# Routed experts on 23 tiles of gathered rows, in place of all eight experts over all tokens

## The reference

```python
# attention: 16 heads of 16, rope, each query picks 4 of 16 key blocks, softmax, RMS per head, @ Wo.T
# feed-forward over T = 1024 tokens, E = 8 experts, K = 2, H = 176
scores = softmax(x @ gate_w)
topk_w, topk_idx = top_k(scores, K)
comb = zeros((T, E)).at[arange(T)[:, None], topk_idx].add(topk_w)
g = silu(einsum('td,edh->teh', x, w_gate)) * einsum('td,edh->teh', x, w_up)
routed = einsum('teh,ehd,te->td', g, w_down, comb)
shared = silu(x @ sw_gate) * (x @ sw_up) @ sw_down      # width 352
out = routed + shared
```

## Time and profile before

| | us |
|---|---|
| median of the 3 runs shown | 426.15 (424.23 to 426.80) |
| span of the profiled execution, first to last instruction | 422.4 |
| layer 0's share of it, to the first transfer issue of layer 1 | 318.9 |
| TensorE, VectorE, POOL, ScalarE busy | 348.9, 300.3, 172.9, 170.7 |
| mean granted clock of TensorE, share of full | 0.935 |
| moved by transfers | 30.2 MB |

### The profile page before, as it was taken

One profiled execution on the slowest core, in us unless ns is written; L12 is line 12 of the kernel. 1 busy time (PEld: TensorE's weight loads), 2 busy tenths in 40 slices (PEclk: granted clock), 3 DMA queues, 4 the chain that ended last, 5 costly groups with the idle time before them and its releaser, 6 DMA issues. The chain is left out here.

```text
span 422.4 us, 6057 instructions
## 1 busy us (share of the span) xinstructions
PE 348.9 (83%) x2028; PEld 240.3 (57%) x2028; DVE 300.3 (71%) x857; ACT 170.7 (40%) x305; POOL 172.9 (41%) x119
## 2 busy tenths in 40 slices
PE   0697767668779989999999999999682888996881
PEld 0586555546546657676665665656581776444641
DVE  3867489867997877894444764684668859758794
ACT  1422453551224323226444445544212475956610
POOL 5654283473444642554256526664536000000023
PEclk9999689697999999999999999999966789999898
DMA  8300168987793311212211141110006100000011
GB/s 267 74 23 21 50 160 178 163 141 182 183 180 88 87 47 44 70 37 52 63 43 42 40 137 39 39 37 2 1 2 216 48 0 2 0 1 0 2 50 50
DMA packets 17009, 30.20 MB, mean 71 GB/s; under 512 B 3140, under 2 KB 12012, under 8 KB 16556
## 3 DMA queue, kind: packets, MB, share of 16 engines
q1 hardware_dynamic: 12946, 18.80, 19.2%
q10 hardware_dynamic: 4032, 11.01, 9.0%
HBM read 24.99 MB, written 4.82 MB: 71 GB/s over the span
## 5 line engine op out<-in xcount | busy, mean ns | idle before, releaser
L388 POOL TENSOR_TENSOR wl<-wr,wh 128x768 fp32r<-128x768 f32 x28 | 51.2, 1829 | 65.3 <-ACT wh L474 49.1
L530 ACT ACTIVATE PT<-bank 128x512 f32<-128x512 f32 (+1 forms) x88 | 44.3, 557 | 39.5 <-PE bank L952 39.4
L687 DVE TENSOR_REDUCE mx<-bank 128x1 f32<-128x384 f32 (+3 forms) x88 | 52.2, 635 | 7.2 <-PE bank L934 6.9
L149 PE MATMUL bank<-xh,wh 128*128 128x512 f32 x112 | 50.7, 452 | 4.0 <-DVE gb L812 1.4
L426 POOL TENSOR_TENSOR gl<-gb,gh 128x512 fp32r<-128x512 f32 x28 | 36.5, 1302 | 37.5 <-DVE gh L819 24.9
L151 PE MATMUL bank<-xh,wl 128*128 128x512 f32 x112 | 45.7, 408 | 0.0
L150 PE MATMUL bank<-xl,wh 128*128 128x512 f32 x112 | 45.5, 407 | 0.0
L933 PE MATMUL bank<-KS,QS 112*128 112x128 bf16 (+3 forms) x128 | 32.9, 310 | 12.5 <-DVE mx L687 6.8
L1213 POOL TENSOR_TENSOR left<-xn,x 128x256 f32<-128x256 f32 x8 | 7.0, 898 | 85.1 <-DVE xn L1440 85.1
L149 PE MATMUL bank<-wh,gh 128*128 128x256 f32 x112 | 36.9, 329 | 0.5 <-POOL gl L426 0.5
L537 ACT ACTIVATE th<-bank 128x512 f32<-128x512 f32 x28 | 16.7, 597 | 45.9 <-PE bank L151 45.8
(11 more groups left out here) (233 smaller groups left out, 824.7 us busy)
## 6 DMA issues: line engine op xcount, KB each, us to landing
wr<-in_w_chunks_dram ACTq DMA_DIRECT2D x28, 384.0 KB, 3.1
KS<-parts_dram SPq DMA_DIRECT2D x12, 256.0 KB, 8.0
parts_dram<-wp SPq DMA_DIRECT2D x12, 128.0 KB
QS<-parts_dram SPq DMA_DIRECT2D x2, 768.0 KB
parts_dram<-x SPq DMA_DIRECT2D x12, 128.0 KB
w_ai<-in_w_ai_dram SPq DMA_DIRECT2D x1, 1152.0 KB, 6.6
x<-in_x_dram SPq DMA_DIRECT2D x2, 512.0 KB, 6.6
QS<-parts_dram SPq DMA_DIRECT2D x2, 512.0 KB
```

The costliest lines, as they stand in the source:

```text
L149: pe.matmul(out, l_hi, r_hi, start=start, stop=False, skip_group_check=skip)
L388: pool.tensor_tensor(wl[:, s % 3, :, :], wr[:, s % 2, :, :], wh[:, s % 3, :, :].bitcast(F32), ALU.subtract).then_inc(wl_ready, 1)
L530: act.activation(PT[:, k % 8, 0:n], bank[k % 2][:, 0:n], ACT.Exp, scale=float(DH) ** -0.5).then_inc(P_ready, 1)
L687: dve.tensor_reduce(mx[:, b * TB + i, heads[0]:heads[-1] + 1], bank[k % 2][:, 0:len(heads) * n].rearrange("p (h n) -> p h n", n=n), AX.X, ...
```

## The change

The router's choice is turned into places on the chip. A token's two experts give it two rows; rows are sorted by expert, each expert's part padded to whole tiles of 128 rows. At most (2048 - 8) / 128 + 8 = 23 tiles arise, and the program always runs 23. Rows (256 values, a destination and a weight) are scattered to DRAM by POOL's indirect transfers (`send_rows`, 16 of them), loaded tile by tile by SP (`load_rows`), transposed, multiplied with their expert's gate and up weights (352 columns at once), and with its down weights; the tile's result is scaled and scattered to `yt_dram` (`send_out`), and all of it is loaded and added at the end (`add_experts`). The expert's weights are found by a register that SP reads (`load_weights`), from a copy in DRAM in another order (`w_dram`), made at the start.

The loop becomes 6 shared steps (0 to 5) and 23 tile steps (6 to 28). Slots are four a step up to step 15 and three after; slots 103 to 112 follow the loop. What was spread to chunk columns is gone (`ksel`, `combT`, L1013). Casts of a tile's weights are ScalarE's before step 16 and VectorE's after, and the scaling of its result likewise; low halves of weights are POOL's, those of rows and hidden values VectorE's. The constants of K for batch 1 are moved behind that batch's stacks. The diff, cut:

```diff
 E, EK, EH, SH = 8, 2, 176, 352
-STEPS = HALVES * CH
+SHARED = HALVES * SCH
+TILES = (B * S * EK - E) // P + E
+STEPS = SHARED + TILES
...
-OUT_SLOT = [next(q for q in range(v[-1] + 1, v[-1] + 4) if q % SLOTS >= 2) for v in SUM_SLOT]
-SLOT_END = OUT_SLOT[-1] + 1
-WO_STEP = 6
+OUT_SLOT = [v[-1] + 2 for v in SUM_SLOT[:-1]] + [SUM_SLOT[-1][-1] + 1]
+SLOT_END = OUT_SLOT[-1] + 4
+WO_STEP = 7
+B_SLOTS = 3
+BIAS_LOAD = 4
+MAX_LOAD = [7, 13]
...
+            for c in range(ECH):
+                sp.dma_start(w_dram[:, :, c * P:(c + 1) * P],
+                             a["w_chunks"][c, :, 0:KD, :].rearrange("p k (s j) -> p (k s) j", s=2)).then_inc(w_placed, 16)
+            def key_constants(b):
                 sp.dma_start(KS[R_BIAS:R_ALL, b, :, :],
-                             spread(a["c_kconst"][:, b * S:(b + 1) * S], 1, H)).then_inc(kconst_ready, 16)
+                             spread(a["c_kconst"][:, b * S:(b + 1) * S], 1, H)).then_inc(kconst_ready[b], 16)
+            key_constants(0)
+            sp.wait_ge(half_done, 2)
+            sp.dma_start(xs_dram.rearrange("(i p) d -> p i d", p=P), spread(xg[:, 0, :], 1, TILES)).then_inc(pad_in, 16)
+            def load_weights(n):
+                first = sp.value_load(expert[0:1, n:n + 1], min_val=0, max_val=(E - 1) * EH)
+                load = SCH + n
+                sp.wait_ge(wh_ready, load - 1)
+                sp.wait_ge(wl_ready, load - 1)
+                if n >= 2:
+                    sp.wait_ge(whd_ready, n - 1)
+                    sp.wait_ge(wld_ready, n - 1)
+                sp.dma_start(wr[:, load % 2, 0:WD].rearrange("p (k j) -> p k j", j=EH),
+                             w_dram[:, :, bass.ds(first, EH)]).then_inc(w_in[load % 2], 16)
+                rows = a["w_chunks"][0:ECH].rearrange("c p k n -> (c p) k n")
+                sp.dma_start(wr[0:EP, load % 2, WD:WT].rearrange("p (h n) -> p h n", h=2),
+                             rows[bass.ds(first, EH), KD, :].rearrange("(h p) n -> p h n", p=EP)
+                             ).then_inc(w_in[load % 2], 16)
+            def load_rows(n):
+                if n >= XBUF:
+                    sp.wait_ge(yt_out[n % XBUF], 16 * (n // XBUF))
+                sp.dma_start(xg[:, n % XBUF, :], xs_dram[n * P:(n + 1) * P, :]).then_inc(xt_in[n % XBUF], 16)
...
             stack_parts(0, range(4))
             stack_bias(0)
-            stack_parts(1, range(4))
-            stack_bias(1)
-            for b in range(B):
-                stack_maxima(b)
+            sp.wait_ge(routed, PLACED)
+            sp.wait_ge(w_placed, 16 * ECH)
+            for n in range(2):
+                load_weights(n)
+            stack_parts(1, range(2))
+            sp.wait_ge(xs_sent, 16 * EK * T)
+            for n in range(XBUF):
+                load_rows(n)
+            stack_parts(1, range(2, 4))
+            key_constants(1)
+            for n in range(2, TILES):
+                load_weights(n)
+                if n >= XBUF:
+                    load_rows(n)
+                if n == BIAS_LOAD:
+                    stack_bias(1)
+                for b in range(B):
+                    if n == MAX_LOAD[b]:
+                        stack_maxima(b)
             sp.wait_ge(PV_done, NG * TB)
             sp.dma_start(xr, a["x"].rearrange("(t p) d -> p t d", p=P)).then_inc(x_again, 16)
+            sp.wait_ge(B_ready, NG * LOADS)
+            for n in range(TILES - XBUF, TILES):
+                sp.wait_ge(yt_out[n % XBUF], 16 * (n // XBUF + 1))
+            src = yt_dram.rearrange("(k t p) d -> p k t d", k=EK, p=P)
+            for k in range(EK):
+                sp.dma_start(yt[:, k], src[:, k]).then_inc(yt_in, 16)
...
+            def split_tile(n):
+                load = SCH + n
+                pool.wait_ge(wh_ready, load + 1)
+                pool.tensor_tensor(tile_w(wl[:, load % 3]), wr[:, load % 2, 0:WD], tile_w(wh[:, load % 3]).bitcast(F32),
+                                   ALU.subtract).then_inc(wl_ready, 1)
+                pool.wait_ge(whd_ready, n + 1)
+                if n < 2:
+                    pool.wait_ge(U_ready, SCH * (n + 1))
+                else:
+                    pool.wait_ge(down_done, SHARED + n - 1)
+                pool.tensor_tensor(down_w(xl, n)[0:EP], wr[0:EP, load % 2, WD:WT], down_w(xh, n)[0:EP].bitcast(F32),
+                                   ALU.subtract).then_inc(wld_ready, 1)
+            def send_rows(k, t):
+                pool.indirect_dma_start(xs_dram, bass.IndirectOffsetOnAxis(ap=place[:, k, t:t + 1], axis=0),
+                                        xe[:, t, :], None, bounds_check=TILES * P - 1,
+                                        oob_is_err=False).then_inc(xs_sent, 16)
+            def send_out(n):
+                pool.wait_ge(ty_ready, n + 1)
+                pool.indirect_dma_start(yt_dram, bass.IndirectOffsetOnAxis(
+                    ap=xg[:, n % XBUF, D:D + 1].bitcast(I32), axis=0), ysb[:, n % 2, :], None,
+                    bounds_check=EK * T * P - 1, oob_is_err=False).then_inc(yt_out[n % XBUF], 16)
...
+                if 1 <= s <= 4:
+                    k = (s - 1) // 2
+                    if s == 1:
+                        pool.wait_ge(pad_in, 16)
+                    pool.wait_ge(routed, LABELLED[k])
+                    for t in range((s - 1) % 2 * TB, (s - 1) % 2 * TB + TB):
+                        send_rows(k, t)
+                if s == SHARED - 1:
+                    split_tile(0)
+            for s in range(SHARED, STEPS):
+                i = s - SHARED
+                if i + 1 < TILES:
+                    split_tile(i + 1)
+                if i:
+                    send_out(i - 1)
...
+            def rows_out(n):
+                act.wait_ge(down_done, SHARED + n + 1)
+                if n >= 2:
+                    act.wait_ge(yt_out[(n - 2) % XBUF], 16 * ((n - 2) // XBUF + 1))
+                act.activation(ysb[:, n % 2, :], bank[7][:, 0:D], ACT.Copy,
+                               scale=xg[:, n % XBUF, D + 1:D + 2]).then_inc(ty_ready, 1)
...
+            def expert_places():
+                dve.wait_ge(rank_ready, 1)
+                rank = bank[5][:, 0:T * E].rearrange("p (t e) -> p t e", e=E)
+                link(dve.tensor_copy(cnt[:, 0, :], bank[5][:, T * E:T * E + E]))
+                link(dve.tensor_tensor(pl[:, 0, :, :], spread(cnt[:, 0, :], 2, E), spread(thr[:, :], 1, E), ALU.is_gt))
+                link(dve.tensor_reduce(cnt[:, 1, :], pl[:, 0, :, :], AX.X, ALU.add))
+                link(dve.tensor_tensor_scan(cnt[:, 2, :], ones8[:, :], cnt[:, 1, :], 0.0, ALU.mult, ALU.add))
...
+            def gathered_lo(n):
+                dve.wait_ge(xh_ready, 2 * B + n + 1)
+                dve.tensor_tensor(tile_x(xl, n), bank[4][:, 0:D], tile_x(xh, n).bitcast(F32),
+                                  ALU.subtract).then_inc(xl_ready, 1)
+            def hidden_lo(n):
+                dve.wait_ge(gh_ready, SHARED + n + 1)
+                dve.tensor_tensor(tile_g(gl, n), bank[6][0:EP, 0:2 * P], tile_g(gh, n).bitcast(F32),
+                                  ALU.subtract).then_inc(gTl_ready, 1)
+            def split_tile(n):
+                load = SCH + n
+                dve.wait_ge(w_in[load % 2], 32 * (load // 2) + 16 * (load % 2))
+                dve.wait_ge(G_ready, SHARED + n - 2)
+                dve.tensor_copy(tile_w(wh[:, load % 3]), wr[:, load % 2, 0:WD]).then_inc(wh_ready, 1)
+                dve.wait_ge(down_done, SHARED + n - 1)
+                dve.tensor_copy(down_w(xh, n)[0:EP], wr[0:EP, load % 2, WD:WT]).then_inc(whd_ready, 1)
+            def rows_out(n):
+                dve.wait_ge(down_done, SHARED + n + 1)
+                dve.wait_ge(yt_out[(n - 2) % XBUF], 16 * ((n - 2) // XBUF + 1))
+                dve.tensor_scalar(ysb[:, n % 2, :], bank[7][:, 0:D], xg[:, n % XBUF, D + 1:D + 2], None,
+                                  ALU.mult).then_inc(ty_ready, 1)
...
+            def add_experts(n):
+                half = y[:, n * TB:(n + 1) * TB, :]
+                dve.wait_ge(yt_in, 16 * EK)
+                link(dve.tensor_tensor(half, half, yt[:, 0, n * TB:(n + 1) * TB, :], ALU.add))
+                dve.tensor_tensor(half, half, yt[:, 1, n * TB:(n + 1) * TB, :], ALU.add).then_inc(y_read, 1)
...
+            for s in range(SHARED, STEPS):
+                i = s - SHARED
+                qs = step_slots(s)
+                if i:
+                    hidden_lo(i - 1)
+                dve.wait_ge(th_ready, SHARED + i + 1)
+                link(dve.scalar_tensor_tensor(out=s2[:, 0:EH], in0=th[:, 0:EH], scalar=1.0, in1=bank[3][:, 0:EH],
+                                              op0=ALU.add, op1=ALU.mult))
+                if i < 2:
+                    dve.wait_ge(gh_ready, SHARED)
+                    dve.wait_ge(gl_ready, SHARED)
                 else:
-                    dve.scalar_tensor_tensor(out=gb[:, :], in0=s2[:, :], scalar=0.5, in1=bank[4][:, :],
```

(57 more changed lines are left out.)

485 lines of the change are left out of this document (316 added, 169 removed).

## The result

The changed kernel takes 458.64 us (median of 4 runs, 456.96 to 463.5) against 425.19 us of the kernel before beside it (4 runs, 423.81 to 426.8): ratio 1.080, 95% interval 1.075 to 1.085, slower. The forecast was 441, with 410 to 456 as its range: the sign was right, the size was not, and the time lies just outside.

A forecast was written before the change was run, and what follows sets the result against it. Transfers were taken to bound the kernel to 106 us, VectorE to 127, TensorE to 302. Sum: 422.4 + 1 + 13 + 16 - 7 - 18 + 10 = 437.4, plus 3.7 carried: 441 us; eight in ten 410 to 456.

The forecast's parts named there:

- What bounds the kernel now: Whole kernel before the change: transfers through SP's queue bound it to 106 us, VectorE to 127, TensorE to 302.
- TensorE: 28 old expert steps, 125 us, become 6 shared and 23 tiles, 80 us: 45 us leave TensorE.
- Early, up to step 6: VectorE's added early work is mostly covered by idle time, and early copies through SP cost nothing: +1 us, 9 without cover.
- Rows come late: Gathered rows wait behind the Q stack in SP's queue, landing about 117; tanh of step 6 at 119.3: +13 us.
- Steps 6 and 7: VectorE loses 1.37 us a step and gets 1.52: no gain, 20.6 us again.
- Tile 2's weights: They wait behind the K stack and one-engine K constants, landing at 147 to 148; tanh of step 8 at 155.5: +16 us.
- Steps 8 to 15: VectorE becomes the bound, with 0.45 us a step for the turn: 56.5 us for 63.5, -7 us.
- Steps 16 to the last head: TensorE needs 88 us, plus 0.5 us a tile for turns: 94 for 112.3, -18 us; ends 88 and 104.
- Tail: Expert rows return after the last tile; VectorE waits 5.6 us, then adds: +10 us, between 4 and 14.
- (a): SP's queue does not hold the tiles; others pass the one-engine constant and rows come with the parts: 412 us, chance 0.26.
- (b): Only one of the two holdups, late rows or late tile 2 weights, is there: 425 to 428 us, chance 0.14.
- (c): POOL bounds from step 16, its work and VectorE's SBUF work excluding each other: stretch 104, total 451 us, chance 0.10.

The follow-up runs named there:

- the moved rows: The four loads of gathered rows issued ahead of the stack of Q instead of behind it, against the changed kernel: 459.22 us against 458.64.
- the scaling later: VectorE's scaling of a finished head group five slots behind the copy instead of three, against the changed kernel: 448.86 us, 9.8 under.
- the short splits: POOL subtracts only 16 columns per tile from step 16, omitting some computation, against the 448.86 us kernel with scaling five slots behind: 438.82 us.
- the cast first alone: VectorE's cast put ahead of its wait for the tanh, sums and scaling unmoved, against the 427.72 us kernel (queue edits, fifth row buffer): 427.49 us.

## Why the prediction came out too low

**What bounds the kernel now** was read rightly, three regimes and the queue in the first one.

**TensorE.** 45 us of busy time were to go, 33.8 went. At full clock the stretch from step 16 needed 85.6 us, close to the forecast of 88; in the changed kernel it was 92.5 there, at a clock of 0.92. So 6.9 of the missing 11.2 us are the same work at the lower clock. The granted clock is 0.868 over the span, 0.935 before, and the rest may lie in the gaps of the other stretches in the same way; that isn't worked out here.

**Early, up to step 6.** +1 was forecast, and +2.9 was measured up to step 5. The copies of weights and the filled buffer cost no more than that.

**Rows come late.** The rows landed at 116.1 us where about 117 was forecast, and the tanh of step 6 came at 119.9 for 119.3. The stretch got 11.0 us longer and not 13, which makes up for the 1.9 us too few before it. The mechanism is shown by the moved rows. But the step was put into the sum as +13 on its own, and by the experiments it was worth nothing while tile 2's weights came at 151: the right size for the wrong path.

**Steps 6 and 7; Tile 2's weights.** The tanh of step 8 came at 158.0 for 155.5. Of the delay behind step 6, the one-engine constant holds 10 us and not 16; the rest is the stack of K and, once that is out of the way, the next item of the queue. The sum of the two hold-ups, 29, came out (28.5 measured in the two stretches), because the second term was counted from where the first one ended; without the first, the second would have been that much longer, as the moved rows showed.

**Steps 8 to 15.** -7 was forecast, -7.1 measured, with VectorE the bound, as forecast. That the number fits so closely is in part luck: VectorE was busy for 51.0 us where 53 was forecast, and idle for 5.4 us where 3.6 was.

**Steps 16 to the last head.** This is the step that failed. The forecast was -18, from TensorE's 88 us plus "0.5 us a tile" for the turn, with 104 as the end. At the last transposes the stretch got 3.5 us longer; with the tail, where -8 was forecast, it is +8.5, and these 16.5 us are about all of the error (455.1 against 437.4). The turn itself was not the trouble. Two couplings were: VectorE waits in order for a root that POOL takes behind two splits and a send (9.8 us by the scaling later), and VectorE's products of two SBUF operands stand still while POOL subtracts (up to 10.0 us by the short splits). Both show up at TensorE as gaps and as the lower clock behind them, the 6.9 us above, and the forecast had the stretch at full clock. The trace of before held both: the product of 1.38 us at 299.98, the root of 3.12 us, and, not read for the prediction, what VectorE waited for ahead of its work in K's space (us, times):

```profile
...
  POOL small L393: 8.5, 2
...
```

There TensorE was idle for 0.3 us all the same. That the longer expert steps and the steps' four slots covered it is argued, not tested. The forecast compared busy sums (67 of VectorE, 62 and sends of POOL, 94 of the stretch) and found that they fit, and they did (64.9 and 70.5 in 112.6 us). That one engine's order puts TensorE's next operand behind the other's queue isn't in a sum.

**Tail.** +10 was forecast, +5.0 measured, inside 4 to 14. The mis-sized term is the return of expert rows: their loads are issued at 320.37, 10 us before the adds at 330.66, and the adds wait for nothing.

**Rivals.** (a) and (b) are refuted for the kernel as changed: weights landed at 151, rows at 116. Rival (c) named the right pair of engines and the right stretch, but by a sum of POOL's and VectorE's work, and with its point of decision at sends over 2.4 us. A send takes 1.0 us:

```profile
L512 POOL DMA_INDIRECT yt_dram<-ysb,x x23 | 23.1, 1006 | 10.6 <-DVE ysb L931 7.1
```

By that test (c) was false, and the part of its cost that is the standstill came all the same. That casts hold sends, as the rule cited with it has it, the changed kernel can't tell: no cast of weights overlaps any of its 23 sends in time. The kernel with the cast first alone can, and agrees: 1.46 us for 1.0 where the two begin together.

## What to carry to other kernels

When a change takes work from the bounding engine, don't stop at comparing busy sums of the others with the new length. Write out one step's order on each engine and follow which operand of the bound stands behind which wait; here that was most of the difference between -18 and +3.5 us. Two hold-ups in one queue need not add: here one was worth nothing while the other stood (0.6 us the wrong way), so each must be priced with the other removed. With the transfers spread over engines and moved ahead, the cast first and the SBUF work last in a step, the routed experts give 418.6 us for 425.3. So placement and one more buffer gave back all of the 33 us that the change had lost. Of these moves only the split of the constants was tried on the kernel before (425.23 us), so what the experts alone are worth between two kernels placed with equal care isn't shown.

## What the runs showed that had not been expected

An issue on SP can be held for 17.69 us behind a transfer of 304 KB on one engine, and is not held (0.63 us) behind the same bytes in 16 and 3 rows. A VectorE product of 0.42 us lasted 3.12 us beside POOL's subtractions and is listed as busy all that time. An indirect send of 128 rows takes POOL 1.0 us, and 1.46 with a cast of VectorE begun 0.07 us behind it; its landing took some 13 us while the DMA engines were full, and SP waited 12.1 us of these for its buffer.
